# Adapter and conditional linear on one core: the up projection wholly from rounded parts, and a new order of work on four engines

## The chip, the cores and the metric

The kernel runs on one core of a Trainium2 chip. The metric is the device time of one execution in microseconds (us); smaller is better. Engines are named as in the profile: PE (TensorE, matrix products), PEld (its weight loads), DVE (VectorE), ACT (ScalarE), POOL (GpSimd), SP (SyncE, which here only issues DMAs). A q behind the name is the engine's own instruction queue.

## What is computed

For each of 32 samples x (512 tokens by 512 features), with weights picked by two id tables:

```
h      = relu(x @ W1[lang] + b1[lang])              # 512 -> 128, "up"
y      = x + h @ W2[lang] + b2[lang]                # 128 -> 512, "down"
normed = (y - mean(y)) * rsqrt(var(y) + 1e-5)
x1     = x + normed * gamma[lang] + beta[lang]
out    = x1 + x1 @ W[cat] + b[cat]                  # "linear"
```

## The kernel before

One sample is in work per step and three samples are in flight: step k does the adapter (up, relu, down, y, its sums) of sample k, the norm, its turning (transposes) and x1 of sample k-1, and the linear of sample k-2; it also prepares x and the adapter's weights of sample k+1 and splits W of sample k-1. There are steps 0 and 1 by hand, steps 2 to 31 from `step`, and an end. The class `Step` numbers the samples and the semaphore counts; `k.count(per, back, more)` is `per` times the index of sample k-back, plus `more`.

**Products by rounded parts.** An fp32 operand is split into a rounded part ("hi", type fp32r, made by ACT with a copy) and the remainder ("lo", made by POOL or DVE with a subtraction). `split_product` (lines 826 to 830) then issues three fp32r matmuls, hi by hi, hi by lo, lo by hi. The linear (12 matmuls for each of four token tiles, `linear_tile` at line 877), down (12, line 868) and the first NS = 3 of the four chunks of up (9, `up` at line 851) are done so. The fourth chunk of up is one plain fp32 matmul on the raw data, line 859, which the trace records as two.

**Order on each engine.** There is no planner: the five instruction lists are written out by hand and every wait is a semaphore. An engine works strictly in its own order. For step k:

- PE (line 889): linear tiles 0, 1 (sample k-2), up (k), turn norm chunks 0, 1 (k-1), linear tile 2, down (k), turn 2, 3 (k-1), linear tile 3. Linear tile 0 of a step waits, chunk by chunk, for x1T_lo of its sample (line 884), which DVE made in the step before.
- ACT (line 545): W's rounded half 0, four norms (k-1), W's half 1, relu (k) in two instructions (lines 518 and 521), two x-quad DMA issues for sample k+2, x1T_hi chunks 0, 1, then the hi parts of W2, W1 and x of sample k+1 (lines 476, 538, 543), squares 0 to 2 (line 527), x1T_hi 2, 3, square 3, the root (line 532).
- DVE (line 739): turn x of k+1 in four instructions (line 659) with outputs 0 and 1 (k-2) between, x1 0, the lo part of h, x1 1, x1T_lo 0, 1 (line 724), output 2, y and means of tiles 0, 1 and of 2, 3 (lines 673, 679), x1 2, 3, x1T_lo 2, 3, output 3, the variance and the inverse root in Newton steps (lines 691 to 710).
- POOL (line 387): identity added to W (line 395), b2 added to x tiles 0, 1 (line 413), W's lo half 0 (line 418), b2 on tiles 2, 3, W's lo half 1, the lo parts of W2, W1, x (lines 372, 378, 384).
- SP (line 276): three id loads into registers, two x-quad issues for k+2, then, behind a wait for the squares of sample k-1, W1 and W2 of k+1, W of k, b2 and x of k+1, b of k-1, half a store, and behind a wait for x1T_lo of k-1 the params (gamma, beta, b1) of k+1, and the other half store.

Relu of sample k waits for its params (line 515), since b1 is in them. The first square of a sample waits for y and its mean on DVE (lines 525, 526), the norms of a sample for its inverse root (line 485).

Of the kernel before, what the change touches and what calls it, by code (L numbers as in the profile page):

```python
# [36 lines left out]
def adapter_then_conditional_linear(nc, x, lang_ids, cat_ids, W1, b1, W2, b2, gamma, beta, W, b, out):  # L37
# [23 lines left out]
    P = 128  # L61
# [3 lines left out]
    NS = 3  # L65
# [17 lines left out]
    with ctx:  # L83
# [14 lines left out]
        b2_bc = [sb(f"b2_bc{i}", [P, H]) for i in range(2)]  # L98
# [34 lines left out]
        zeros = sb("zeros", [P, P])  # L133
        spare = sb("spare", [P, 4])
        ids = sb("ids", [1, 2, S], I32)
        param_rows = norm[0:L, :, :]
        param_table = sb("param_table", [P, L, NP])
# [7 lines left out]
        neg_mean_copy, var_eps, newton, newton2 = (d_bank[1][:, n * NT:(n + 1) * NT] for n in range(4))  # L145

# [85 lines left out]
        def _(sp):  # L232
# [3 lines left out]
            def load_x_quads(s, p, quads=(0, 1)):  # L236
# [17 lines left out]
            def load_b2(lang, p):  # L254
                sp.dma_start(b2_bc[p][:, :], b2[bass.ds(lang, 1)].to_broadcast([P, H])
                             ).then_inc(b2_in[p], 16)
# [19 lines left out]
            def step(h, p, quads=True, loads=True, w_load=True, turn=True, linear=True):  # L276
# [7 lines left out]
                if turn:  # L284
                    cat_b = sample_id(1, k.sample(1), G)
                if quads:
# [40 lines left out]
            load_b2(lang1, 1)  # L327
# [10 lines left out]
            load_x_quads(2, 0, range(NQ))  # L338
# [11 lines left out]
            last = Step(S // ROUND, 3)  # L350
            store(last, 2, 0)
# [10 lines left out]
        def _(pool):  # L362
# [24 lines left out]
            def step(h, p, adapter=True, turn=True, follow=True):  # L387
# [11 lines left out]
                def plus_b2(t):  # L399
# [5 lines left out]
                    pool.tensor_tensor(x_tok[p][:, t, :], x_tok[p][:, t, :], b2_bc[p][:, :],  # L405
                                       ALU.add).then_inc(x_b2_done, 1)

                def plus_b2_pair(t):
# [4 lines left out]
                    pool.tensor_tensor(pair, pair, b2_bc[p][:, :].rearrange("p (o h) -> p o h", o=1  # L413
# [56 lines left out]
        def _(act):  # L470
# [107 lines left out]
            def load_x_quads(s, p):  # L578
                for n in (2, 3):
                    act.dma_start(x_quad[p][quad(n), :, :],  # L580
                                  x_quads[bass.ds(s, 1), n].rearrange("o j b f -> j (o b) f")
# [416 lines left out]
```

## Time and profile before

| | us |
|---|---|
| median of 3 runs (lowest, highest) | 616.76 (616.46, 617.0) |
| profiled execution, its own time | 616.09 |
| span of that execution | 614.3 |
| PE busy | 607.1 (99%) |
| DVE, ACT, POOL busy | 523.2, 512.8, 524.0 |
| granted TensorE clock | 1.000 |

The span is counted from the first to the last instruction; 1.8 us of the time lie around it. Busy shares are averages over 32 samples, and a step repeats every 18.40 us, so the rows below are mostly those of one step in the middle (335.5 to 353.9 us). Each timeline row gives start, duration, engine and line, operation, operands, count, and in brackets the idle time ahead of it with what ended it. The same instruction returns 18.40 us later in the next step.

### The profile page before, as it was taken

The page shows a single profiled execution, that of the slowest core. Times are in us where ns is not written, and L with a number is a line of the kernel's source. Part 1 is how long each engine was busy: PE and PEld are TensorE (multiplying, and loading weights), DVE is VectorE, ACT ScalarE, POOL GpSimd, SP SyncE. Part 2 cuts the span into 40 slices and gives each one's busy share as a digit, 9 for nine tenths or more (in the row PEclk, how much of TensorE's full clock was granted, in tenths as well). Part 3 has the DMA queues.
Part 4 walks back from the last instruction along what each step waited for, and adds up shares of the span by engine and source line. Part 5 has one row for each costly group of instructions (what it writes and reads, how often), then busy time and mean ns, then how long its engine had stood idle before and what let it go on. Part 6 is the DMA issues. An engine that isn't in the chain of part 4 may idle for free.

```text
span 614.3 us, 10766 instructions
## 1 busy us (share of the span) xinstructions
PE 607.1 (99%) x2888; PEld 492.3 (80%) x2888; DVE 523.2 (85%) x1154; ACT 512.8 (83%) x769; POOL 524.0 (85%) x262
## 2 busy tenths in 40 slices
PE   9999999999999999999999999999999999999998
PEld 7767888888877888888888888888888888888887
DVE  1799899889799898898988998888898988998673
ACT  4768889889888889888989889889888989889770
POOL 4789999899889899889999888898988999888830
PEclk9999999999999999999999999999999999999999
DMA  9968998897997988989888998988998888998422
GB/s 308 247 206 272 307 305 275 278 296 250 307 297 251 301 271 281 318 270 292 274 287 280 306 297 258 287 280 273 313 290 280 281 287 275 300 306 276 154 85 104
DMA packets 125759, 166.24 MB, mean 271 GB/s; under 512 B 10882, under 2 KB 72588, under 8 KB 121632
## 3 DMA queue, kind: packets, MB, share of 16 engines
q1 hardware_dynamic: 94756, 150.12, 75.2%
q10 hardware_dynamic: 30972, 15.78, 9.2%
q8 instruction: 11, 0.18, 0.1%
q14 instruction: 20, 0.16, 0.1%
HBM read 132.17 MB, written 33.55 MB: 270 GB/s over the span
## 4 chain that ended last, share of the span: by engine, by line
PE 93%; DMA 2%; ACT 2%; DVE 2%; issue 1%; SPq 0%; POOL 0%; DVEq 0%; POOLq 0%; ACTq 0%
PE o_bank L828 18%; PE o_bank L830 18%; PE o_bank L829 18%; PE n_bank L846 9%; PE d_bank L828 5%; PE d_bank L830 5%; PE d_bank L829 5%; PE d_bank L859 5%; PE y_bank L828 2%; PE y_bank L830 2%; PE y_bank L829 2%; DMA x_tok<-in_x 2%; ACT norm L491 1%; PE y_bank L836 1%; DVE xT L659 1%
## 5 line engine op out<-in xcount | busy, mean ns | idle before, releaser
L828 PE MATMUL o_bank<-w_hi,x1T_hi 128*128 128x512 f32 x512 | 205.3, 401 | 0.8 <-DVE x1T_lo L724 0.8
L830 PE MATMUL o_bank<-w_hi,x1T_lo 128*128 128x512 f32 x512 | 200.0, 391 | 0.0
L829 PE MATMUL o_bank<-w_lo,x1T_hi 128*128 128x512 f32 x512 | 199.1, 389 | 0.0
L418 POOL TENSOR_TENSOR w_lo<-w_raw,w_hi 128x1024 fp32r<-128x1024 f32 x62 | 149.4, 2409 | 9.9 <-ACT w_hi L501 9.9
L659 DVE STREAM_TRANSPOSE xT<-x_quad 128x512 f32<-128x512 f32 x120 | 127.2, 1106 | 31.1 <-DMA x_quad<-in_x 31.1
L491 ACT ACTIVATE norm<-y,neg_mean_rstd,rstd 128x512 f32<-128x512 f32 x127 | 151.1, 1264 | 1.1 <-DVE neg_mean_rstd L709 1.1
L413 POOL TENSOR_TENSOR x_tok<-x_tok,b_bc 128x1024 f32<-128x1024 f32 x60 | 145.4, 2424 | 1.2 <-issue 1.1
L830 PEld LDWEIGHTS o_bank<-w_hi,x1T_lo 128*128 128x128 f32 x512 | 96.1, 188 | 21.0
L508 ACT ACTIVATE x1T_hi<-n_bank,params 128x512 fp32r<-128x512 f32 x126 | 84.6, 689 | 33.6 <-DVE n_bank L718 26.4
L828 PEld LDWEIGHTS o_bank<-w_hi,x1T_hi 128*128 128x128 f32 x512 | 96.3, 188 | 19.6 <-issue 1.7
L829 PEld LDWEIGHTS o_bank<-w_lo,x1T_hi 128*128 128x128 f32 x512 | 96.4, 188 | 17.8
L527 ACT ACTIVATE x_tok<-y,neg_mean 128x512 f32<-128x512 f32 x128 | 91.7, 718 | 17.4 <-DVE neg_mean L679 17.4
L384 POOL TENSOR_TENSOR xs_lo<-xT,xs_hi 128x1536 fp32r<-128x1536 f32 x29 | 102.1, 3522 | 0.0
L718 DVE SCALAR_TENSOR_TENSOR n_bank<-n_bank,params,xT 128x512 f32<-128x512 f32 x126 | 92.4, 757 | 10.3 <-PE n_bank L846 9.9
L724 DVE SCALAR_TENSOR_TENSOR x1T_lo<-n_bank,params,x1T_hi 128x512 fp32r<-128x512 f32 x126 | 90.8, 749 | 9.4 <-ACT x1T_hi L508 4.2
L736 DVE TENSOR_TENSOR out_half<-o_bank,b_bc 128x512 f32<-128x512 f32 x127 | 86.0, 677 | 11.8 <-PE o_bank L830 11.7
L501 ACT ACTIVATE w_hi<-w_raw 128x1024 fp32r<-128x1024 f32 x64 | 67.5, 1057 | 18.1 <-POOL w_raw L395 17.2
L372 POOL TENSOR_TENSOR w_lo<-w_raw,w_hi 128x512 fp32r<-128x512 f32 x31 | 40.4, 1303 | 47.6 <-ACT w_hi L476 47.6
L846 PEld LDWEIGHTS n_bank<-ident,norm 128*128 128x128 f32 x504 | 59.4, 145 | 9.0 <-ACT norm L491 1.1
L846 PE MATMUL n_bank<-ident,norm 128*128 128x128 f32 x504 | 65.7, 273 | 0.1
L395 POOL TENSOR_TENSOR w_raw<-w_raw,ident 128x512 f32<-128x512 f32 x32 | 50.5, 1577 | 0.0
L828 PE MATMUL d_bank<-xs_hi,w_hi 128*128 128x512 f32 x87 | 46.0, 529 | 0.0
(87 smaller groups left out, 821.2 us busy)
## 6 DMA issues: line engine op xcount, KB each, us to landing
w_raw<-in_L_cond_W SPq DMA_DIRECT2D x32, 1024.0 KB, 6.5
out<-out_half SPq DMA_DIRECT2D x63, 512.0 KB, 4.1
x_tok<-in_x SPq DMA_DIRECT2D x31, 1024.0 KB, 11.3
w_raw<-in_L_cond_W SPq DMA_DIRECT2D x64, 256.0 KB, 4.1
b_bc<-in_L_cond_b SPq DMA_DIRECT2D x64, 256.0 KB, 8.5
x_quad<-in_x SPq DMA_DIRECT2D x62, 256.0 KB, 3.7
x_quad<-in_x ACTq DMA_DIRECT2D x58, 256.0 KB, 10.7
x_tok<-in_x ACTq DMA_DIRECT2D x2, 256.0 KB, 3.3
```

Of the source, the lines that this page charges most:

```text
L384: pool.tensor_tensor(xs_lo[:, :, :], xT[(k.x + 1) % 3][:, 0:NS, :], xs_hi[:, :, :].bitcast(F32), ALU.subtract).then_inc(xs_lo_done, 1)
L413: pool.tensor_tensor(pair, pair, b2_bc[p][:, :].rearrange("p (o h) -> p o h", o=1).to_broadcast([P, 2, H]), ALU.add).then_inc(x_b2_done, 2)
L418: pool.tensor_tensor(w_lo[q][:, c:c + 2, :], w_raw[q][:, c:c + 2, :], w_hi[q][:, c:c + 2, :].bitcast(F32), ALU.subtract).then_inc(w_lo_don ...
L491: act.activation(dst, src, ACT.Identity, scale=rstd[:, t:t + 1], bias=neg_mean_rstd[:, t:t + 1]).then_inc(norm_done, 1)
L527: act.activation(x_tok[k.b][:, t, :], y[:, t, :], ACT.Square, bias=neg_mean[:, t:t + 1], accum_out=sq_sum[:, t:t + 1]).then_inc(sq_done, 1)
L659: dve.transpose(xT[(k.x + 1) % 3][:, c, :].rearrange("p (b j) -> p b j", j=SQ), x_quad[1 - k.b][:, :, c::NC]).then_inc(xT_done, 1)
L718: dve.scalar_tensor_tensor(norm_bank(k, c)[:, :], norm_bank(k, c)[:, :], params[q][:, c:c + 1], xT[(k.x + 2) % 3][:, c, :], ALU.mult, ALU. ...
L724: dve.scalar_tensor_tensor(x1T_lo[q][:, c, :], norm_bank(k, c)[:, :], params[q][:, NC + c:NC + c + 1], x1T_hi[q][:, c, :].bitcast(F32), AL ...
L828: pe.matmul(acc, lhs_hi, rhs_hi, start=first, stop=False)
L829: pe.matmul(acc, lhs_hi, rhs_lo, start=False, stop=False)
L830: return pe.matmul(acc, lhs_lo, rhs_hi, start=False, stop=last)
L846: ins = pe.transpose(norm_bank(k, c)[:, t * P:(t + 1) * P], norm[:, t, c * P:(c + 1) * P] if by_chunk(k) else norm[:, t, c::NC], ident[:, :])
```

## The change

- All four chunks of up go by rounded parts (NS = 4): the fp32 matmul becomes three fp32r ones, and the hi and lo parts of W1 and x are a third larger.
- ACT: three norms come ahead of W's half 0 and the fourth ahead of half 1; the hi part of W2 comes ahead of relu, those of x and W1 between relu and x1T_hi 0; the four squares and the root come ahead of x1T_hi 2 and 3. ACT issues no x quads.
- DVE: variance and inverse root come ahead of x1T_lo 2, 3 and output 3.
- POOL: both b2 additions come ahead of W's lo halves, the first also ahead of the identity; the lo part of x comes ahead of that of W1.
- SP: issues all four x quads; params of sample k are loaded in step k, behind W and x (before: in step k-1); the half store moves on to the next step; b2 has one buffer and is loaded last, after POOL has added the b2 of sample k. The steps have four id loads instead of three.
- `zeros` (used by the idle matmuls of the start) lies in an output buffer.

```diff
-    NS = 3
+    NS = 4
...
-        b2_bc = [sb(f"b2_bc{i}", [P, H]) for i in range(2)]
+        b2_bc = sb("b2_bc", [P, H])
...
-        zeros = sb("zeros", [P, P])
+        zeros = out_half[1][:, 1, 0:P]
...
+        def b2_of(k):
+            return b_bc[1] if k.since(1) and not k.since(2) else b2_bc
... SP, load_x_quads
-                for n in quads:
+                for n in range(NQ):
... SP, step
+                if w_load and k.since(2):
+                    lang_now = sample_id(0, k.sample(0), L)
                 if quads:
                     sp.wait_ge(xT_done, k.count(NC, 0, NC))
                     load_x_quads(k.sample(-2), p)
...
                     load_w(cat_w, p)
                 if loads:
-                    load_b2(lang, q)
                     load_x(k.sample(-1), q)
+                if w_load and k.since(2):
+                    sp.wait_ge(x1_lo_done, k.count(NC, 1, 0))
+                    load_params(lang_now, p)
+                if linear and k.since(3):
+                    store(k, 3, 1)
                 if turn:
...
                 if linear:
                     store(k, 2, 0)
                 if loads:
-                    sp.wait_ge(x1_lo_done, k.count(NC, 0, 0))
-                    load_params(lang, q)
-                if linear:
-                    store(k, 2, 1)
+                    sp.wait_ge(x_b2_done, k.count(NT, 0, NT))
+                    load_b2(lang, q)
... POOL, step
+                    if adapter and not k.last(2):
+                        plus_b2_pair(0)
                     if turn:
                         plus_identity()
-                    if adapter:
+                    if adapter and k.last(2):
                         plus_b2_pair(0)
-                    if turn:
-                        low_w_pair(0)
                     if adapter:
                         plus_b2_pair(2)
                     if turn:
+                        low_w_pair(0)
                         low_w_pair(2)
                 if follow:
                     low_w2(q, k.count(1, -1, 1))
                     if k.since(2):
+                        low_xs(k)
                         low_w1(k)
-                        low_xs(k)
... ACT, step
-                if k.last(2):
-                    for t in range(NT):
-                        normalise(k, t)
-                    high_w(k, 0)
-                else:
-                    high_w(k, 0)
-                    for t in range(NT):
-                        normalise(k, t)
+                for t in range(NT - 1):
+                    normalise(k, t)
+                high_w(k, 0)
+                normalise(k, NT - 1)
                 high_w(k, 2)
+                if follow:
+                    high_w2_of_next(k)
                 if adapter:
                     relu(k)
-                if follow and not k.last(S - 2):
-                    load_next_x_quads(k)
+                if follow:
+                    high_xs_of_next(k)
+                    high_w1_of_next(k)
                 high_x1(k, 0)
                 high_x1(k, 1)
-                if follow:
-                    high_w2_of_next(k)
-                    high_w1_of_next(k)
-                    high_xs_of_next(k)
                 if adapter:
-                    square(k, 0)
-                    square(k, 1)
-                    square(k, 2)
+                    for t in range(NT):
+                        square(k, t)
+                    deviation(k)
                 high_x1(k, 2)
                 high_x1(k, 3)
-                if adapter:
-                    square(k, 3)
-                    deviation(k)
... DVE, step
                 x1(k, 3)
+                if adapter:
+                    variance(k)
+                    inverse_deviation(k)
                 low_x1(k, 2)
                 low_x1(k, 3)
                 output(k, 3)
-                if adapter:
-                    variance(k)
-                    inverse_deviation(k)
... PE, up
-                                        False, c == parts - 1)
+                                        c == 0 and parts == NC, c == parts - 1)
```

## Rows read from the trace of the kernel before

**Rows 1.** One step in the middle, windows view: busy time of each engine

```profile
335.51:353.91 18.40, 18.40 (x88) 14.99 (x88) 17.59 (x39) 16.23 (x25) 16.72 (x9) 1.00 0.89 285
```

The columns are the stretch, its length, then PE, PEld, DVE, ACT and POOL busy with instruction counts, the granted clock, the DMA share and GB/s.

**Rows 2.** Timeline of PE in that step: up, and the turning behind it

```profile
335.34 1.02 PE L859 MATMUL d_bank<-xT,w_raw 128*128 128x512 f32 x2
...
336.43 0.39 PE L829 MATMUL d_bank<-xs_lo,w_hi 128*128 128x512 f32 x1
...
338.28 1.03 PE L846 MATMUL n_bank<-ident,norm 128*128 128x128 f32 x8
```

**Rows 3.** Groups over the span: operands, count, busy us, mean ns

```profile
L384 POOL TENSOR_TENSOR xs_lo<-xT,xs_hi 128x1536 fp32r<-128x1536 f32 x29 | 102.1, 3522 | 0.0
...
L543 ACT ACTIVATE xs_hi<-xT 128x1536 fp32r<-128x1536 f32 x29 | 43.0, 1481 | 0.0
...
L378 POOL TENSOR_TENSOR w_lo<-w_raw,w_hi 128x384 fp32r<-128x384 f32 x29 | 29.6, 1020 | 0.0
```

**Rows 4.** Timeline of ACT in that step

```profile
338.48 0.66 ACT L518 ACTIVATE d_bank<-d_bank,params 128x512 f32<-128x512 f32 x1 [0.17 <-PE d_bank L830]
339.17 0.60 ACT L521 ACTIVATE hT_hi<-d_bank 128x512 fp32r<-128x512 f32 x1
...
340.66 1.27 ACT L508 ACTIVATE x1T_hi<-n_bank,params 128x512 fp32r<-128x512 f32 x2 [0.89 <-DVE n_bank L718]
341.82 0.63 ACT L476 ACTIVATE w_hi<-w_raw 128x512 fp32r<-128x512 f32 x1
342.34 0.52 ACT L538 ACTIVATE w_hi<-w_raw 128x384 fp32r<-128x384 f32 x1
342.75 1.49 ACT L543 ACTIVATE xs_hi<-xT 128x1536 fp32r<-128x1536 f32 x1
344.77 0.72 ACT L527 ACTIVATE x_tok<-y,neg_mean 128x512 f32<-128x512 f32 x1 [0.53 <-DVE neg_mean L679]
...
349.09 0.30 ACT L532 ACTIVATE std<-sq_sum,eps 128x4 f32<-128x4 f32 x1
349.90 1.06 ACT L501 ACTIVATE w_hi<-w_raw 128x1024 fp32r<-128x1024 f32 x1 [0.51 <-POOL w_raw L395]
```

**Rows 5.** Timeline of ACT in the last adapter step, which prepares no next sample

```profile
577.69 0.66 ACT L518 ACTIVATE d_bank<-d_bank,params 128x512 f32<-128x512 f32 x1 [0.18 <-PE d_bank L830]
...
580.41 0.69 ACT L508 ACTIVATE x1T_hi<-n_bank,params 128x512 fp32r<-128x512 f32 x1 [0.66 <-DVE n_bank L718]
583.86 0.72 ACT L527 ACTIVATE x_tok<-y,neg_mean 128x512 f32<-128x512 f32 x1 [2.76 <-DVE neg_mean L679]
```

**Rows 6.** Timeline of DVE in the step of the middle, its end

```profile
347.74 1.41 DVE L724 SCALAR_TENSOR_TENSOR x1T_lo<-n_bank,params,x1T_hi 128x512 fp32r<-128x512 f32 x2
...
349.79 0.17 DVE L700 RECIPROCAL r<-std 128x4 f32<-128x4 f32 x1
...
350.60 0.16 DVE L709 TENSOR_TENSOR neg_mean_rstd<-d_bank,rstd 128x4 f32<-128x4 f32 x1
```

**Rows 7.** DMA view of stretches that hold one issue: W late alone, then x, b

```profile
w_raw<-in_L_cond_W SPq DMA_DIRECT2D x1, 1024.0 KB, 4.8
...
x_tok<-in_x SPq DMA_DIRECT2D x1, 1024.0 KB, 10.5
...
b_bc<-in_L_cond_b SPq DMA_DIRECT2D x1, 256.0 KB, 10.8
```

The last column is the time from issue to landing in us; W was issued at 572.92, x at 337.86 and b at 338.46.

**Rows 8.** Windows view: W, b and a store without x quads, then two stretches with x quads

```profile
575.00:579.00 4.00, 4.00 (x22) 3.24 (x21) 1.21 (x2) 3.77 (x5) 4.00 (x3) 1.00 1.01 403
337.30:343.30 6.00, 6.00 (x32) 4.98 (x31) 5.73 (x9) 4.91 (x9) 4.32 (x3) 1.00 1.06 329
...
22.00:24.00 2.00, 1.10 (x9) 0.86 (x7) 0.86 (x2) 1.73 (x3) 2.00 (x3) 1.00 1.16 240
```

**Rows 9.** Timelines of the start: SP's first quads of step 2, ACT's relu of sample 2

```profile
39.77 0.87 SPq L238 DMA_DIRECT2D x_quad<-in_x  x2
...
41.94 0.66 ACT L518 ACTIVATE d_bank<-d_bank,params 128x512 f32<-128x512 f32 x1 [1.45 <-PE d_bank L859]
```

More of the change, by code:

```diff
@@ L234, in sample_id, with load_x_quads @@
                 return sp.value_load(ids[0:1, which, bass.ds(s, 1)], min_val=0, max_val=count - 1)
-            def load_x_quads(s, p, quads=(0, 1)):
-                for n in quads:
+            def load_x_quads(s, p):
+                for n in range(NQ):
                     sp.dma_start(x_quad[p][quad(n), :, :],
@@ L252, in load_w2, with load_b2 @@
                              ).then_inc(w2_in[p], 16)
-            def load_b2(lang, p):
-                sp.dma_start(b2_bc[p][:, :], b2[bass.ds(lang, 1)].to_broadcast([P, H])
+            def load_b2(lang, p, dst=b2_bc):
+                sp.dma_start(dst[:, :], b2[bass.ds(lang, 1)].to_broadcast([P, H])
                              ).then_inc(b2_in[p], 16)
@@ L326, in _ @@
             lang1 = sample_id(0, 1, L)
-            load_b2(lang1, 1)
+            load_b2(lang1, 1, b_bc[1])
             load_w1(lang1, 1)
@@ L336, in _ @@
             load_params(lang1, 1)
-            load_x_quads(2, 0, range(NQ))
+            load_x_quads(2, 0)
             step(0, 1, linear=False)
@@ L350, in _ @@
             last = Step(S // ROUND, 3)
+            store(last, 3, 1)
             store(last, 2, 0)
@@ L404, in plus_b2 @@
                             pool.wait_ge(first_xT_turned, k.count(NC, 0, NC))
-                    pool.tensor_tensor(x_tok[p][:, t, :], x_tok[p][:, t, :], b2_bc[p][:, :],
+                    pool.tensor_tensor(x_tok[p][:, t, :], x_tok[p][:, t, :], b2_of(k)[:, :],
                                        ALU.add).then_inc(x_b2_done, 1)
@@ L412, in plus_b2_pair @@
                     pair = x_tok[p][:, t:t + 2, :]
-                    pool.tensor_tensor(pair, pair, b2_bc[p][:, :].rearrange("p (o h) -> p o h", o=1
+                    pool.tensor_tensor(pair, pair, b2_of(k)[:, :].rearrange("p (o h) -> p o h", o=1
                                        ).to_broadcast([P, 2, H]), ALU.add).then_inc(x_b2_done, 2)
@@ L547, in step @@
                 k = Step(h, p)
-                if k.last(2):
-                    for t in range(NT):
-                        normalise(k, t)
-                    high_w(k, 0)
-                else:
-                    high_w(k, 0)
-                    for t in range(NT):
-                        normalise(k, t)
+                for t in range(NT - 1):
+                    normalise(k, t)
+                high_w(k, 0)
+                normalise(k, NT - 1)
                 high_w(k, 2)
+                if follow:
+                    high_w2_of_next(k)
                 if adapter:
                     relu(k)
-                if follow and not k.last(S - 2):
-                    load_next_x_quads(k)
+                if follow:
+                    high_xs_of_next(k)
+                    high_w1_of_next(k)
                 high_x1(k, 0)
                 high_x1(k, 1)
-                if follow:
-                    high_w2_of_next(k)
-                    high_w1_of_next(k)
-                    high_xs_of_next(k)
                 if adapter:
-                    square(k, 0)
-                    square(k, 1)
-                    square(k, 2)
+                    for t in range(NT):
+                        square(k, t)
+                    deviation(k)
                 high_x1(k, 2)
                 high_x1(k, 3)
-                if adapter:
-                    square(k, 3)
-                    deviation(k)
[L578 to L581, printed above, removed]
-                                  ).then_inc(xq_in[p], 16)
-            def load_next_x_quads(k):
-                act.wait_ge(xT_done, k.count(NC, 0, NC))
-                load_x_quads(k.sample(-2), k.b)
             act.dma_start(x_tok[0][:, 1, :], x_rows[0, :, 1, :]).then_inc(first_x_in[1], 16)
@@ L627, in _ @@
             high_w2_of_next(k1)
-            load_next_x_quads(k1)
             for p in range(2, 2 + ROUND):
@@ L642, in _ @@
             STATS = 5
-            dve.memset(zeros[:, :], 0.0).then_inc(zeros_done, 1)
+            dve.memset(zeros, 0.0).then_inc(zeros_done, 1)
             dve.memset(spare[:, 0:1], 0.0).then_inc(out_done, OUT_CREDIT)
@@ L835, in keep_clock @@
                 for _ in range(count):
-                    pe.matmul(idle_bank[:, 0:P], zeros[:, :], zeros[:, :], start=True, stop=True)
+                    pe.matmul(idle_bank[:, 0:P], zeros, zeros, start=True, stop=True)
             def turn_norm(k, c):
```

## The prediction, made before the changed kernel ran

> **What bounds the kernel now.** I read the windows view of one step first, then the timelines of PE, ACT and DVE in that step, the groups, and last the DMA view. In the step of the middle PE is busy for all of its 18.40 us, while ACT has 16.23 us of work and POOL 16.72 [rows 1]. So a step costs what PE's list costs, and every other engine has a gap that costs nothing. ACT's gaps are the brackets of [rows 4]: 0.17 us for up, 0.89 for x1, 0.53 for the first mean, 0.51 for W with the identity. The question for a reordering is whether each engine's waits still fit into a step once its order is another. The profiled execution took 616.09 us against a median of 616.76; my sum is made against 616.09, and 0.2% (some 1.2 us) is about what a measurement of this kernel can tell from no change.
>
> **PE.** The fp32 chunk starts at 335.34; the first lo-matmul behind it starts at 336.43, which holds the chunk and one fp32r matmul. From 336.43 to the turning at 338.28 eight fp32r matmuls start, 0.231 us each [rows 2]. The chunk thus costs 1.09 - 0.23 = 0.86 us, its three fp32r matmuls 0.69. PE's list becomes 18.40 - 0.86 + 0.69 = 18.23 us: 0.17 less in each of 29 steps (3 to 31), 4.9 us if PE stays the bound.
>
> **ACT and POOL work.** Rounding 1536 columns of x takes 1.481 us [rows 3] and 384 of W1 0.52 [rows 4], so 0.84 ns a column; 512 and 128 more columns cost 0.43 + 0.11 = 0.54 us. ACT has then 16.23 + 0.54 = 16.77 us of work. On POOL the slope is (3.522 - 1.020)/1152 = 2.17 ns a column [rows 3], 640 more cost 1.39 us, and POOL has 18.11 us of work, just under PE's 18.23. POOL overlaps its instructions slightly, which the busy time of [rows 1] already holds.
>
> **The gap on ACT that loses its filler.** This is the largest term. The first square of a sample waits for its mean. That mean is behind x1T_lo 1, output 2 and two y tiles on DVE, and x1T_lo 1 waits for x1T_hi 1 on ACT. In [rows 4] x1T_hi 1 ends at 341.93 and the first square starts at 344.77, 2.84 us later. Before, ACT spends 2.3 us of this with the hi parts of W2, W1 and x, and only 0.53 shows as idle. The last step, which prepares no sample, shows the bare gap: from x1T_hi 1 at 580.41 to the square at 583.86, with 2.76 us idle [rows 5]. The change moves all three fillers ahead of x1T_hi 0 and puts nothing in their place; DVE's order between x1T_lo 1 and the mean stays. All of ACT's list lies on one closed loop (square, root, x1T_hi 2 and 3, norms, relu, hi parts, x1T_hi 0 and 1, gap, next square), so a step cannot be shorter than 16.77 + 2.84 = 19.6 us, whatever PE does. That excludes a gain unless one of the two numbers is wrong.
>
> **The loop through PE is a little longer.** Count from S, the end of the fourth square. The root ends 0.32 later (square's end 349.07 to root's end 349.39 [rows 4]). The inverse chain takes 0.97 from 349.79 to 350.76 [rows 6] and is now ahead of x1T_lo 2 and 3, whose two instructions take 1.41 [rows 6]: 0.32 + 0.05 + 0.97 + 1.41 = S + 2.75. Linear tile 0 of the next step then has its last three matmuls (0.69), tile 1 has 12 (2.77 at 0.231; I take 2.73, since such tiles run slightly faster than up), up has 12 (2.77), and 0.2 until relu starts: S + 9.15. ACT itself is there at S + 0.3 + 1.25 (x1T_hi 2, 3) + 6.8 (norms and W's two halves: 349.90 to the relu at 338.48 + 18.40 less its wait of 0.17) + 0.52 (W2) = S + 8.9, so PE's path is last by about 0.3.
>
> From relu to the next S: relu in two instructions 1.29, x 1.40 + 0.43, W1 0.41 + 0.11 (starts of neighbours in [rows 4]), x1T_hi 0 and 1 1.27, the gap 2.84, four squares 3.1 (344.77 to 349.09, less 1.25 for the x1T_hi 2 and 3 between them). That is 10.8, and the step 9.15 + 10.8 = 19.9 us. The cost on PE appears as a wait of linear tile 0 for x1T_lo 2, about 19.9 - 18.2 = 1.7 us a step. Slack elsewhere: the b2 buffer is released when POOL has added it, half a step ahead of the next use; x quads are issued from SP some 6 us after the last stores and needed a step later; output 3 ends as tile 1 needs its bank, with about 0.1 us to spare. I cost these at nothing; if one cover fails it adds its excess to the same loop, at most a few tenths. The wait of DVE for x quads disappears into slack. Taking the quad issues off ACT saves nothing, since they lay in its wait. The reordered POOL waits fit, as POOL has 1.8 us to spare in 19.9. The granted clock stays 1.00 even where PE worked 1.10 of 2.00 us [rows 8], so I add nothing for it.
>
> **The params.** SP now issues the params of sample k in step k, behind W1, W2, W and x of its own queue, and the W1 issue waits for the squares of k-1 (S). Relu of k waits for these params. In front of them lie 2.5 MB (2.62 million bytes). W alone landed 4.8 us after its issue [rows 7]; at the 403 GB/s of [rows 8] its 1.05 million bytes take 2.6, which leaves 2.2 of latency. So the params land at S + 0.05 + 2.2 + 6.5 = S + 8.75 at that rate, and at S + 10.2 at the 329 GB/s of the mixed stretch [rows 8]. I take the first, since x quads, which make the mixed stretches slow, have then landed; it is 0.4 ahead of PE's path, so it costs nothing in a steady step. The upper end would make the step 10.2 + 0.05 + 10.8 = 21.1. That a small transfer doesn't pass a large one of its queue I take from x and b: issued at 337.86 and 338.46 they landed at 348.4 and 349.3 [rows 7].
>
> The Trainium skill, page "DMA: Bandwidth & Descriptors", section "Queues, rings and completion order", says that on each engine descriptors are consumed in ring order, but also that completion is "not FIFO per issuing engine". By the first the sum is as above; by the second the params could come early, and only the next term would fall away. That the landings of x and b kept their order agrees with the first.
>
> **Once, at the start.** Step 2 has no lead: SP issues the quads of sample 4 at 39.77 when DVE has turned sample 2 [rows 9], now four of them, then W1, W2, W, x and only then the params of sample 2. Before, these had long landed and relu of sample 2 ran at 41.94 [rows 9]. Now 1.05 million bytes of quads at 240 GB/s (4.4 us; a stretch with many quads, [rows 8]), 2.62 million at 403 (6.5) and 2.2 latency put it at 52.9: 10.9 us later. Bounds: 9.3 with all at 403 GB/s, 11.5 with all at 329, nothing if params overtake.
>
> **Sum.** Relu of sample 2 to that of sample 31 is 577.69 - 41.94 = 535.75 us for 29 steps, 18.47 each. New: 29 x 19.9 = 577.1, 41.4 more. Behind the last relu PE has up finished about 0.5 us sooner relative to it. 616.1 + 10.9 + 41.4 - 0.5 = 667.9; I say 668.
>
> **Rivals.** (a) The params cycle decides: relu at S + 10.2 or later, steps of 20.5 to 21.1 us, 616.1 + 10.9 + 29 x (20.5 to 21.1 - 18.47) = 686 to 703. For it: most stretches of the trace are below 403 GB/s, and SP may be late. Against: those stretches are mixed with quads. 0.27. (b) The params overtake x (the page's second rule as it would act here): no loss at the start, steps of 19.6 to 19.9, so 616.1 + 33 to 41 = 649 to 657. Against it is the order of x and b. 0.08. (c) Faster: the swap in up decides, because the gap at the first square is covered. It wins if that gap is under 18.23 - 16.77 = 1.46 us instead of 2.84; the price is the 0.17 us of a step, and the time 616.1 - 4.9 = 611. For it: PE is the bound now and gets shorter, and the inverse root comes earlier. Against: [rows 5], where nothing but DVE's own list lies in the gap. 0.05. (d) Gap as in (c), but POOL's 18.11 us meet a wait and the step becomes 18.6: 620. 0.02.
>
> **How the numbers follow.** The forecast has 0.57 (660 to 680), (a) 0.27, (b) 0.08, (c) 0.05, (d) 0.02, the rest 0.01 beyond. The range reaches from 649, steps of 19.6 without the loss at the start, to 703, steps of 21.1 with it. Faster 0.05, within 0.2% 0.01, slower 0.94.
>
> **What would show it.** Right: steps of 19.9 us, ACT idle some 2.8 us in each ahead of the first square, waiting for the mean; PE idle 1.5 to 2 us a step at linear tile 0, waiting for x1T_lo; relu of sample 2 near 53 us with a wait for the params' DMA. Relu waiting for that DMA in every step is (a). An ACT without a wait of over 1.5 us ahead of the squares, and steps of 18.2, would prove the argument wrong.

## The result and the profile after

The changed kernel takes 747.0 us (742.41 to 750.75, 4 runs) against 616.63 us (616.46 to 617.0) before: 1.210 times as long [1.207, 1.214]. The forecast was 668 and the range ended at 703. The direction was right; the size was not. The profiled execution took 743.29 us, 127.2 more than the one of before, at a mean granted clock of 0.968.

Read first where the added time lies. Relu of sample 2 starts at 54.00 us (41.94 before), relu of sample 31 at 704.71. So 12.1 us are lost once at the start, and the 29 steps are (704.71 - 54.00)/29 = 22.44 us each against 18.47, which is 115.0 us. Together that is all but 0.2 of the 127.2; the rest lies behind the last relu. The page of the kernel after gives the busy times, and in its second fence line the shares of the chain that ended last:

```profile
PE 643.5 (87%) x2917; PEld 505.8 (68%) x2917; DVE 526.3 (71%) x1154; ACT 519.1 (70%) x769; POOL 561.9 (76%) x262
...
DMA 32%; ACT 23%; DVE 19%; PE 13%; issue 12%; SPq 1%; ACTq 0%; DVEq 0%
```

PE was busy for 99% of the span and is so for 87% now; PE's own work is only 13% of the chain. The largest share is DMA, all of it one item: the params. The waits, over the span (total us, times, longest), tell what this is:

```profile
ACT d_bank L528 <- DMA params<-param_table: 88.8, 27, 4.8
...
ACT x_tok L537 <- DVE neg_mean L669: 85.8, 31, 2.8
...
PE o_bank L818 <- DVE x1T_lo L714: 62.6, 30, 2.3
```

Line 528 is relu. It waits for the params in 27 of 32 samples, which the forecast had as rival (a). The second line is the gap ahead of the first square, the third is linear tile 0. One step on ACT, from relu to relu:

```profile
325.15 0.66 ACT L528 ACTIVATE d_bank<-d_bank,params 128x512 f32<-128x512 f32 x1 [3.68 <-DMA params<-param_table]
...
332.76 0.73 ACT L537 ACTIVATE x_tok<-y,neg_mean 128x512 f32<-128x512 f32 x1 [2.84 <-DVE neg_mean L669]
...
335.82 0.30 ACT L542 ACTIVATE std<-sq_sum,eps 128x4 f32<-128x4 f32 x1
...
343.99 0.61 ACT L486 ACTIVATE w_hi<-w_raw 128x512 fp32r<-128x512 f32 x1
347.32 0.66 ACT L528 ACTIVATE d_bank<-d_bank,params 128x512 f32<-128x512 f32 x1 [2.71 <-DMA params<-param_table]
```

Two stretches make the step. From relu to the end of the fourth square, S = 335.80, it is 10.65 us, and the gap of 2.84 us stands in it as forecast. From S to the next relu it is 11.52 us instead of 9.15. ACT is idle for the last 2.71 of these, and what ends the wait is the landing of the params. (PE too is late in this step, see the paragraph on the clock below.) SP's queue in the same step shows what is ahead of them:

```profile
335.95 0.36 SPq L251 DMA_DIRECT2D w_raw<-in_L_cond_W  x1
336.40 0.38 SPq L255 DMA_DIRECT2D w_raw<-in_L_cond_W  x1
336.97 0.33 SPq L267 DMA_DIRECT2D w_raw<-in_L_cond_W  x1
337.39 0.39 SPq L247 DMA_DIRECT2D x_tok<-in_x  x1
338.57 0.53 SPq L263 DMA_DIRECT2D params<-param_table  x1
339.36 1.01 SPq L277 DMA_DIRECT2D out<-out_half  x1
```

W1, W2, W and x go out within 1.8 us of S; the params go out at S + 2.8, when x1T_lo is ready. The DMA view of stretches that hold one of these issues each (last column: us to landing) gives their landings, and the chain names the one that ends last:

```profile
w_raw<-in_L_cond_W SPq DMA_DIRECT2D x1, 1024.0 KB, 6.9
...
x_tok<-in_x SPq DMA_DIRECT2D x1, 1024.0 KB, 9.7
...
params<-param_table SPq DMA_DIRECT2D x1, 4.5 KB, 8.7
```

```profile
338.57 8.66 DMA params<-param_table
```

x landed at 337.39 + 9.7 = 347.1, and the 4.5 KB of params at 338.57 + 8.66 = 347.2, that is S + 11.4: they land with the burst. So it is in all 27 steps that load an x: the params land 0.15 to 0.21 us behind it. The windows view says at what rate the burst came in:

```profile
336.00:337.20 1.20, 0.00 (x0) 0.00 (x0) 0.91 (x6) 1.20 (x4) 1.20 (x2) 1.00 0.00 0
...
337.60:347.20 9.60, 9.27 (x39) 7.60 (x39) 6.93 (x10) 7.00 (x7) 7.88 (x5) 0.82 0.94 312
...
339.00:341.50 2.50, 2.50 (x8) 1.95 (x7) 2.50 (x4) 2.50 (x3) 1.36 (x1) 0.60 0.86 246
...
343.00:344.50 1.50, 1.50 (x8) 1.22 (x7) 1.38 (x2) 1.50 (x3) 1.50 (x2) 1.00 0.83 202
344.50:347.10 2.60, 2.60 (x16) 2.21 (x15) 0.05 (x1) 0.10 (x1) 2.60 (x2) 1.00 1.04 383
```

No byte moves before 337.2. From about 337.4 to 347.1 the engines bring in the 2.62 million bytes, which is 270 GB/s; with the half store issued behind they move 312 in all, at 94% of their time. The forecast had 403 GB/s. The rate is uneven: 246 GB/s behind the landing of W2 (339.3), 202 around that of W (343.9), and 383 at the end, when W has landed and x is still on its way. This step is one of the quicker ones: over the span x takes 10.3 us to land (median), and the params land at S + 12.1 (median; 10.4 to 12.5 in the steps that load an x).

### The profile page after: what moved, and what is told of

Read it like the earlier page. It is cut to its first block, busy times and chain, and to the rows that moved or that the text cites. A ratio compares the mean times of both kernels' runs of the same rounds, so it can differ in the third digit from the quotient of the medians.

```text
span 741.5 us, 10909 instructions
## 1 busy us (share of the span) xinstructions
PE 643.5 (87%) x2917; PEld 505.8 (68%) x2917; DVE 526.3 (71%) x1154; ACT 519.1 (70%) x769; POOL 561.9 (76%) x262
## 4 chain that ended last, share of the span: by engine, by line
DMA 32%; ACT 23%; DVE 19%; PE 13%; issue 12%; SPq 1%; ACTq 0%; DVEq 0%
DMA params<-param_table 32%; ACT x_tok L537 7%; DVE x1T_lo L714 7%; ACT xs_hi L553 6%; DVE y L663 5%; DVE out_half L726 3%; ACT d_bank L528 3%; PE o_bank L818 2%; ACT x1T_hi L518 2%; PE o_bank L819 2%; PE o_bank L820 2%; ACT w_hi L548 2%; ACT std L542 1%; PE d_bank L849 1%; DVE r L690 1%
## 5 line engine op out<-in xcount | busy, mean ns | idle before, releaser
L818 PE MATMUL o_bank<-w_hi,x1T_hi 128*128 128x512 f32 x512 | 215.2, 420 | 62.6 <-DVE x1T_lo L714 62.6
L820 PE MATMUL o_bank<-w_hi,x1T_lo 128*128 128x512 f32 x512 | 206.7, 404 | 0.0
L819 PE MATMUL o_bank<-w_lo,x1T_hi 128*128 128x512 f32 x512 | 206.2, 403 | 0.0
L393 POOL TENSOR_TENSOR xs_lo<-xT,xs_hi 128x2048 fp32r<-128x2048 f32 x29 | 133.7, 4609 | 86.0 <-ACT xs_hi L553 86.0
L537 ACT ACTIVATE x_tok<-y,neg_mean 128x512 f32<-128x512 f32 x128 | 91.5, 716 | 85.8 <-DVE neg_mean L669 85.8
L819 PEld LDWEIGHTS o_bank<-w_lo,x1T_hi 128*128 128x128 f32 x512 | 100.8, 197 | 17.5
L726 DVE TENSOR_TENSOR out_half<-o_bank,b_bc 128x512 f32<-128x512 f32 x127 | 85.8, 676 | 13.9 <-PE o_bank L820 13.8
L528 ACT ACTIVATE d_bank<-d_bank,params 128x512 f32<-128x512 f32 x32 | 21.2, 662 | 98.2 <-DMA params<-param_table 88.8
L518 ACT ACTIVATE x1T_hi<-n_bank,params 128x512 fp32r<-128x512 f32 x126 | 79.1, 678 | 5.0 <-DVE n_bank L708 4.9
L836 PE MATMUL n_bank<-ident,norm 128*128 128x128 f32 x504 | 72.0, 278 | 0.1
L836 PEld LDWEIGHTS n_bank<-ident,norm 128*128 128x128 f32 x504 | 57.6, 145 | 19.1 <-DVE x1T_lo L714 13.7
L654 DVE TENSOR_TENSOR hT_lo<-d_bank,hT_hi 128x512 fp32r<-128x512 f32 x32 | 22.1, 692 | 68.0 <-ACT hT_hi L531 67.8
L553 ACT ACTIVATE xs_hi<-xT 128x2048 fp32r<-128x2048 f32 x29 | 55.3, 1905 | 0.0
## 6 DMA issues: line engine op xcount, KB each, us to landing
x_tok<-in_x SPq DMA_DIRECT2D x31, 1024.0 KB, 10.3
```

Of the source, the lines that this page charges most:

```text
L393: pool.tensor_tensor(xs_lo[:, :, :], xT[(k.x + 1) % 3][:, 0:NS, :], xs_hi[:, :, :].bitcast(F32), ALU.subtract).then_inc(xs_lo_done, 1)
L537: act.activation(x_tok[k.b][:, t, :], y[:, t, :], ACT.Square, bias=neg_mean[:, t:t + 1], accum_out=sq_sum[:, t:t + 1]).then_inc(sq_done, 1)
L726: dve.tensor_tensor(out_half[t // 2][:, t % 2, :], o_bank[t % 2][:, :], b_bc[k.b][:, :], ALU.add).then_inc(out_done, 1)
L818: pe.matmul(acc, lhs_hi, rhs_hi, start=first, stop=False)
L819: pe.matmul(acc, lhs_hi, rhs_lo, start=False, stop=False)
L820: return pe.matmul(acc, lhs_lo, rhs_hi, start=False, stop=last)
```

## The experiments

Read the results with this table. The profiled execution of each kernel is about 38 us, plus the start of relu of sample 2, plus 29 steps. Start and mean step are from relu's rows of that execution, whose own time can lie some us from the median (743.3 against 747.0 for the changed kernel). Relu is line 523, 526 or 529 in kernels whose lines have moved.

| | us (median) | relu 2 | step | ratio to before |
|---|---|---|---|---|
| before | 616.6 | 41.94 | 18.47 | 1 |
| after | 747.0 | 54.00 | 22.44 | 1.210 [1.207, 1.214] |
| params early | 667.0 | 48.38 | 20.02 | 1.084 [1.078, 1.090] |
| params early, NS = 3 | 658.7 | 48.52 | 19.68 | 1.068 [1.064, 1.071] |
| params between W and x | 669.4 | 50.89 | 20.00 | one run |
| params by ACT's queue | 709.8 | 49.07 | 21.44 | one run |
| gap filled, params late | 707.4 | 54.57 | 21.18 | one run |
| both mended | 645.6 | 49.08 | 19.23 | 1.044 [1.038, 1.050] |
| both, NS = 3 | 642.7 | 48.32 | 19.15 | 1.042 [1.038, 1.045] |
| both, identity first | 642.7 | 48.52 | 19.09 | 1.042 [1.040, 1.045] |
| all edits | 616.8 | 47.91 | 18.29 | 1.000 [0.999, 1.001] |
| all edits, start mended | 613.9 | 41.95 | 18.38 | 0.995 [0.994, 0.997] |
| all edits but params late | 731.2 | 53.69 | 22.05 | one run |

**Theory A**: two loops stacked on ACT's list, the params behind the burst and under them the gap ahead of the first square. **Rival B**: everything is on one queue, so moving 4.5 KB within it changes little. **Rival C**: the gap alone decides.

### Params ahead of W and x

```diff
                     load_w2(lang, q)
+                if w_load and k.since(2):
+                    sp.wait_ge(x1_lo_done, k.count(NC, 1, 0))
+                    load_params(lang_now, p)
                 if w_load:
...
                     load_x(k.sample(-1), q)
-                if w_load and k.since(2):
-                    sp.wait_ge(x1_lo_done, k.count(NC, 1, 0))
-                    load_params(lang_now, p)
```

> The changed kernel, with SP issuing the params of the step ahead of W and x instead of behind them. Theory A (the closed loop through the params transfer is the bound: squares of k-1 to the landing of the params of k 12 us, relu of k to its squares 10.6): relu no longer waits for a DMA; the step falls from 22.8 us to what PE's path gives, 19.9 if the granted clock stays at 1.00, 21.3 if it drops to 0.5 behind each wait as in the trace of the changed kernel; time about 668 to 710. Rival B (one DMA queue instead of two makes all loads slow and that is what is paid): the step stays at 22 us or more, about 740.

Measured: 667.0 us (666.26 to 672.4), 80 less, from moving one issue past two others. In the trace of this run the DMA view, and relu in two neighbouring steps:

```profile
params<-param_table SPq DMA_DIRECT2D x31, 4.5 KB, 1.7
```

```profile
330.17 0.66 ACT L528 ACTIVATE d_bank<-d_bank,params 128x512 f32<-128x512 f32 x1 [0.56 <-PE d_bank L820]
...
350.13 0.66 ACT L528 ACTIVATE d_bank<-d_bank,params 128x512 f32<-128x512 f32 x1 [0.57 <-PE d_bank L820]
```

The params land 1.7 us after their issue instead of 9.3, relu waits for PE alone, and the step is 19.96 us (mean 20.02). That is the step of the forecast's main case within about 0.1 us: it had assumed that the params cost nothing in a steady step and worked out 19.9. Rival B falls.

### Gap filled, params left late

```diff
                     relu(k)
+                high_x1(k, 0)
+                high_x1(k, 1)
                 if follow:
                     high_xs_of_next(k)
                     high_w1_of_next(k)
-                high_x1(k, 0)
-                high_x1(k, 1)
```

> The changed kernel, with ACT making x1T_hi 0 and 1 ahead of the hi parts of x and W1 of the next sample, so that these lie in its gap ahead of the first square; params still late. Theory A (both loops run through ACT's gap, so its filler shortens the params' loop too): relu to squares 10.6 less 2.3 = 8.3 us, plus 12 to the params, steps of 20.3 us, about 675. Theory C (ACT's unfilled gap alone explains the loss): steps of 18.2 to 18.6, about 611 to 622.

Measured: 707.41 us. In the waits of this run relu's wait for the params stays, and the gap is gone from ACT's timeline:

```profile
ACT d_bank L528 <- DMA params<-param_table: 71.7, 29, 4.9
```

```profile
550.43 0.73 ACT L537 ACTIVATE x_tok<-y,neg_mean 128x512 f32<-128x512 f32 x1 [0.44 <-DVE neg_mean L669]
```

Relu to S is 9.2 us there (544.27 to 553.48) instead of 10.65, but S to relu is 12.5. The gap alone is worth some 40 us of 130, so rival C falls; and the loop through the params bounds this kernel at 21.2 us a step. I had expected steps of 20.3 and 675 in all, a miss. Relu to S came out 0.9 us above the 8.3 expected, and 0.85 of this is a wait that the fillers used to hide. It now shows ahead of x1T_hi 1, for DVE's x1 1, which stands behind the lo part of h:

```profile
546.99 0.69 ACT L518 ACTIVATE x1T_hi<-n_bank,params 128x512 fp32r<-128x512 f32 x1 [0.85 <-DVE n_bank L708]
```

### Both, and both with up as before

The two diffs above together; then also `NS = 3`, which gives up its plain fp32 chunk back. That second kernel tells whether the swap in up is worth anything here.

> Both edits: params ahead of W and x, and ACT's gap filled. Theory A: no loop but PE's own list is left, steps of 18.23 us, and 611 to 614, if POOL's 18.11 us of work meet no wait; if POOL waits for the hi part of x, steps of 18.4 to 18.8, 617 to 628. Rival B: above 640.

> The two edits again, with NS back to 3: one chunk of up is plain fp32, and the hi and lo parts are a quarter smaller. If PE is the bound in both, this is 0.17 us a step slower than the kernel with both edits, by 4.9 us (0.8%); if POOL's list is the bound there, this one is faster than it, near 616.

Measured: 645.59 us (640.19 to 646.12) and 642.66 us (640.72 to 643.56). Both sit at steps of 19.2, well above PE's list (18.23 us, with NS = 3 18.40) and well above what was expected. The 2.9 us between their medians lie within their spreads, so the pair shows nothing for or against the swap in up while this loop is the bound. The two-by-two of these four kernels is: params alone -80, gap alone -40, both -101. The edits don't add, because each takes away one loop and the next longest takes over. The chain of the run with both edits names the third, here from one landing to the next:

```profile
297.94 9.48 DMA out<-out_half
...
307.51 0.08 DVE out_half L726
...
308.12 1.30 DVE y L663 x4
...
310.21 0.84 ACT x_tok L537 x3
...
314.53 0.75 DVE x1T_lo L714
...
315.40 0.51 SPq L263
...
317.26 9.05 DMA out<-out_half
```

The half store is issued behind the params (L263, which hold SP until x1T_lo is done), W and x, and takes 9 us to land. DVE can't write output 2 of the next step until it has, y stands behind output 2 in DVE's list, and the squares behind y. This item has 38% of the chain. The order of the same queue is at fault again, with the store in the place of the params, and the prediction did not have it.

### Identity ahead of b2 on POOL

```diff
-                    if adapter and not k.last(2):
-                        plus_b2_pair(0)
                     if turn:
                         plus_identity()
-                    if adapter and k.last(2):
+                    if adapter:
                         plus_b2_pair(0)
```

> The kernel with both edits (645.6 us, steps of 18.9), with POOL adding the identity to W ahead of b2 on tiles 0 and 1, as before the change. If the loop that is left runs through POOL (lo part of x, lo part of W1, b2, identity, W's hi half 0, norms, relu, hi part of x), it is 2.4 us shorter, and the next one decides, root to relu through PE 9.15 us and relu to squares 9.3: steps of 18.5, about 634. If the loop isn't there: no change within 0.3%.

Measured: 642.67 us (640.73 to 644.09), within the spread of the kernel it starts from. ACT's wait for POOL did vanish (9.5 us over 20 steps before the edit, 0.7 after) and bought nothing that can be told from the spread: a wait off the chain. The half store kept 35% of the chain. A miss.

### All edits

On top of that, three together: DVE does x1 1 ahead of the lo part of h; SP issues the half store ahead of W and x; in step 2 the hi part of W2 goes behind relu.

```diff
                     load_params(lang_now, p)
+                if linear and k.since(3):
+                    store(k, 3, 1)
                 if w_load:
...
                     load_x(k.sample(-1), q)
-                if linear and k.since(3):
-                    store(k, 3, 1)
...
-                if follow:
+                if follow and not k.last(2):
                     high_w2_of_next(k)
                 if adapter:
                     relu(k)
+                if follow and k.last(2):
+                    high_w2_of_next(k)
...
                 x1(k, 0)
+                x1(k, 1)
                 if adapter:
                     low_h(k)
-                x1(k, 1)
```

> As the run with the identity first, and besides: DVE makes x1 chunk 1 ahead of the lo part of h (ACT waits 0.67 us for it ahead of x1T_hi 1), SP issues the half store ahead of W and x (DVE waits up to 1.9 us for it), and in step 2 the hi part of W2 comes behind relu (it waits 7 us for its load there). Every loop is then under PE's list of 18.23 us, if I have them all: steps of 18.23, relu of sample 2 back near 42 us, and 611 to 613, 0.6% to 0.9% faster than before the change. If POOL's 18.1 us of work meet a wait: 618 to 625.

Measured: 616.82 us (615.94 to 618.41, 10 runs), ratio 1.000 [0.999, 1.001], some 4 us above the 611 to 613 expected. The steps came out as expected, the start did not. Relu in the middle, and at the start:

```profile
414.35 0.66 ACT L526 ACTIVATE d_bank<-d_bank,params 128x512 f32<-128x512 f32 x1 [0.56 <-PE d_bank L820]
...
432.63 0.66 ACT L526 ACTIVATE d_bank<-d_bank,params 128x512 f32<-128x512 f32 x1 [0.59 <-PE d_bank L820]
```

```profile
47.91 0.66 ACT L526 ACTIVATE d_bank<-d_bank,params 128x512 f32<-128x512 f32 x1 [7.46 <-DMA params<-param_table]
```

The steps are 18.2 to 18.3 us, which is PE's list of 18.23; PE has 95% of the chain and the half store none. Its median landing went from 8.3 to 5.5 us. By the chain it is the store edit that took away the 19.1 us loop, but the three edits were not run apart, so the share of the DVE edit is open. What the steps gain over before (29 x 0.18 = 5 us) the start gives back: relu of sample 2 waits 7.46 us for params that now stand behind four x quads.

### All edits, and the start mended

```diff
+                if w_load and k.last(2):
+                    sp.wait_ge(x1_lo_done, k.count(NC, 1, 0))
+                    load_params(lang_now, p)
                 if quads:
...
-                if w_load and k.since(2):
+                if w_load and k.since(2) and not k.last(2):
```

> The kernel with all edits (616.8 us, steps of 18.25, but relu of sample 2 at 47.9 us instead of 41.9, 7.5 us of it a wait for its params behind the quads), with the params of step 2 issued ahead of the quads of step 2. Relu of sample 2 returns to 41 to 42.5 us, the steps stay at 18.25: 610 to 612, 0.8% to 1.1% faster than before the change. If the loss at the start is made good later by PE's list anyway: no change, 616.8.

Measured: 613.9 us (613.41 to 615.47, 11 runs) against 617.23, ratio 0.995 [0.994, 0.997]. This version is 0.5% faster than the kernel before, and the interval keeps clear of no change. ACT at the start, then the windows view of one step:

```profile
41.95 0.66 ACT L529 ACTIVATE d_bank<-d_bank,params 128x512 f32<-128x512 f32 x1 [1.44 <-PE d_bank L852]
...
47.62 0.63 ACT L487 ACTIVATE w_hi<-w_raw 128x512 fp32r<-128x512 f32 x1 [4.37 <-DMA w_raw<-in_L_cond_W]
...
64.53 0.66 ACT L529 ACTIVATE d_bank<-d_bank,params 128x512 f32<-128x512 f32 x1 [0.52 <-PE d_bank L823]
```

```profile
300.00:318.25 18.25, 18.25 (x90) 15.13 (x89) 16.37 (x38) 16.62 (x25) 18.14 (x10) 1.00 0.95 286
```

Relu of sample 2 is back at its old time. But W2 for sample 3 is late behind the same quads, and that step takes 22.6 us, some 4 more than the others; so the gain is half of what was expected. In the steady step PE has no gap at all, and POOL is busy for 18.14 of 18.25 us: the new order leaves POOL 0.1 us of slack.

### Params late, all else mended

The reverse test: in the kernel with all edits the params go back behind W and x. I expected the params loop at its known length.

> The kernel with all edits, with the params behind W and x again, as in the changed kernel: that one part alone on a kernel whose other loops are short. Squares to params 11.5 to 12.2, relu to squares 8.6: steps of 20.1 to 20.8, with 6 us at the start some 675 to 695. If late params only hurt together with ACT's unfilled gap: steps of 18.3, 623.

Measured: 731.23 us (one run), 114 more from the place of one 4.5 KB load, and 36 above my upper end. Relu, and SP's queue:

```profile
409.78 0.66 ACT L526 ACTIVATE d_bank<-d_bank,params 128x512 f32<-128x512 f32 x1 [4.54 <-DMA params<-param_table]
```

```profile
418.73 0.38 SPq L255 DMA_DIRECT2D w_raw<-in_L_cond_W  x1
421.56 0.41 SPq L277 DMA_DIRECT2D out<-out_half  x1
```

Between the two issues SP is held for 2.4 us by the half store, which waits for output 3. That store is now ahead of W, x and the params in the queue. Relu to S fell to 8.35 us (409.78 to 418.13), and S to relu rose to 13.1 (to 431.25). The edit that mends one order lengthens the loop of another: I had priced the params as if SP's queue ahead of them were unchanged.

### Between W and x, and on ACT's own queue

Two tests of what sets the landing. In the first the params are issued behind W and ahead of x; in the second ACT issues them itself, on its own DMA queue, ahead of W's half 1, and SP no longer does:

```diff
                 normalise(k, NT - 1)
+                if adapter:
+                    lang_now = act.value_load(ids[0:1, 0, bass.ds(k.sample(0), 1)], min_val=0, max_val=L - 1)
+                    act.wait_ge(x1_lo_done, k.count(NC, 1, 0))
+                    act.dma_start(params[k.b][:, :],
...
                 high_w(k, 2)
```

> The changed kernel, with the params between W and x: 1.57 million bytes ahead of them instead of 2.62. If the bytes ahead set the landing (2.3 us and 290 GB/s, as x showed in the changed kernel), they land 7.7 us after the squares, 1.4 ahead of PE's path: no wait for them in a steady step, steps of 19.9 to 20.1, 668 to 675. If it is the whole burst that must end first (as the run on ACT's queue hints): landing 10 us or more after the squares, steps of 21.5 us or more, above 705.

> The changed kernel, with the params of the step issued by ACT ahead of W's half 1 instead of by SP behind W and x; the same transfer at about the same time, on the other queue. Theory A1 (the params are late because their queue serves in order and 2.6 million bytes lie ahead): they land within 2 to 4 us of their issue, relu waits for them under 1 us, steps near 20.3 us, 670 to 690. Rival A2 (the DMA engines are full, so that any transfer issued then waits): landing in 6 us or more after the issue, steps of 22 us or more, above 735.

Measured: 669.4 us with steps of 20.0, and 709.8 us with steps of 21.4. The DMA view of the first and of the second:

```profile
params<-param_table SPq DMA_DIRECT2D x31, 4.5 KB, 5.7
```

```profile
params<-param_table ACTq DMA_DIRECT2D x30, 4.5 KB, 6.8
```

With 1.57 million bytes ahead (W1, W2, W) the landing takes 5.7 us, with 2.62 million 9.3, with W1 and W2 alone 1.7. In each run the params land right behind the last large load ahead of them: 0.2 us behind x in the changed kernel, 0.2 us behind W here (0.15 to 0.32 in the 27 steps), while x lands 2.7 to 4.5 us later. Ahead of W and x they find W1 and W2 nearly in (W2 lands at S + 3.5, they at S + 4.5), and 1.7 us is what is left of a landing. Here they land near S + 8.4, just before PE's path, so this kernel runs like the one with early params. It is the bytes ahead that count, not the queue's length behind. The landing that I had expected was S + 7.7.

A queue of its own saves little: the params issued at 408.53 find W and x already issued on the other queue (W at 405.71, x at 406.14) and land 6.5 us later, 6.8 in the median. They are issued 1.2 us later than SP would (S + 4.0) and land at S + 10.75 instead of S + 12.1. They do get ahead of x: at 415.0 against 415.75 here, and in all 27 steps that load an x, by 0.1 to 1.6 us, where on SP's queue they never did. So neither branch of what was expected holds as it stands: not 2 to 4 us, and not steps of 22. The Trainium skill, page "DMA: Bandwidth & Descriptors", section "Queues, rings and completion order", says that an engine goes round its queues by packets, but also that the semaphore's increment lands only after every earlier write of that engine, across its queues. The first rule alone would let the params land early, and the second can hold them up behind what the engines have already taken in. This trace has a landing ahead of x and yet 6.8 us after the issue, so it shows neither rule acting alone, and no run here separates a late read from a late semaphore.

### Early params with the old up

```diff
-    NS = 4
+    NS = 3
```

> The changed kernel with params early (667.0 us, steps of 19.9), NS back to 3, so that 0.54 us of ACT's rounding (0.43 of it, and the W1 part 0.11, on the loop from relu to the squares) are gone and PE's up is 0.17 longer. If the loop through ACT's unfilled gap is the bound: steps of 19.9 - 0.54 + 0.17 = 19.5, 11 us less, 656. If PE's list decided: 0.17 a step slower, 672.

Measured: 658.7 us (658.05, 659.37), steps of 19.68. As expected, giving up its fp32 chunk back makes this order faster by 8 us (11 expected). PE's list isn't the bound there; the loop is, from relu over ACT's list and its gap to S, and from S over x1T_lo and PE to relu. The swap adds 0.54 us to ACT's part of it and takes 0.17 from PE's. So the swap is a loss as long as this loop is the longer one. Once PE's list is the bound it should be a gain, 18.25 against 18.40 us a step, but the kernel with all edits was not run with NS = 3.

## Why the prediction was wrong in size and right in sign

**PE, ACT and POOL work.** Right. PE's step with nothing in its way is 18.25 us (18.23 forecast), POOL's work 18.14 (18.11), ACT's 16.6 (16.77).

**The gap on ACT.** Right: 2.84 us in the row above, and 85.8 us over 31 squares. With the params out of the way, the loop that holds it gives steps of 20.0.

**The loop through PE.** Right: with early params 19.96 us against 19.9. That this kernel's 667.0 us also meet the 668 is luck: the 668 hold 10.9 us for late params at the start, which it doesn't have. It loses 6.4 us there for another reason (below), and some 3.4 us in 29 steps of 20.02 instead of 19.9. In the kernel after, relu to S took 10.65 us against 10.8.

**The params: the step that failed.** The text had them at S + 8.75, with S + 10.2 as upper end, and called them hidden by 0.4 us. They landed at S + 11.4 in the step above, at S + 12.1 in the median, and the mean step of 22.44 puts relu at S + 11.8 on average. The latency at the head was no error: first bytes came 1.5 us after the first issue, where I had 2.2 in all. The term for the burst was: 2.62 million bytes took 9.7 us, not 6.5. I had taken 403 GB/s from a stretch with W, b and a store, and 329 as the lower bound because a stretch with x quads held it. "The x quads have then landed" was true and didn't help: the burst ran at 270 without them. It is not x that is slow, as the 383 GB/s at its end show, but the stretches behind W2's landing and around W's. The trace of before has a stretch of that kind in the very load that the 403 came from, W issued at 572.92:

```profile
573.50:575.00 1.50, 1.50 (x8) 1.06 (x7) 0.24 (x1) 1.50 (x2) 1.50 (x1) 1.00 0.73 98
```

The first 1.5 us in which it moved bytes ran at 98 GB/s; I had booked them as latency, to be paid once ahead of the burst, and taken the rate from 575.00 on. In the burst such slow stretches lie inside it. What makes them slow no run here separates, so the cause of the low rate stays open. The row at 240 GB/s in [rows 8] was kept for the start alone; had it been the lower bound, the upper end would have been S + 13.2, steps of up to 24 us, and the range would have held the result. And a margin of 0.4 us under a term that ran from 8.75 to 10.2 was no margin. The error is worth (22.44 - 19.9) x 29 = 74 us, and the experiment with early params got back 80 by the medians and 76 between the profiled executions, of which 5.6 lie at the start (54.00 - 48.38) and 70 in the steps.

**Rival (a)** named the right mechanism and its sign, relu waiting for that DMA (27 of 32 samples), with 0.27. Its price carried the same wrong rates: its condition was a landing at S + 10.2 "or later", but its dearest step, 21.1 us, is that of S + 10.2. Rival (b) falls: on SP's queue the params never overtook x. The steps of rivals (c) and (d), 18.2 to 18.6 us, exist only in the kernels with all edits, where the gap is filled and two more loops are cut.

**The clock.** I had added nothing. After PE's idle time of 2.34 us at linear tile 0 it was granted 0.50, the lower of its two levels (1.2 GHz), for some 3 us:

```profile
337.93 0.76 PE L818 MATMUL o_bank<-w_hi,x1T_hi 128*128 128x512 f32 x1 [2.34 <-DVE x1T_lo L714]
338.49 0.63 PE L819 MATMUL o_bank<-w_lo,x1T_hi 128*128 128x512 f32 x1
338.92 0.63 PE L820 MATMUL o_bank<-w_hi,x1T_lo 128*128 128x512 f32 x1
```

```profile
340.00:340.80 0.80, 0.80 (x3) 0.61 (x3) 0.80 (x2) 0.80 (x1) 0.36 (x1) 0.50 0.99 297
```

Its matmuls start 0.43 us apart there instead of 0.23. Up ends 1.6 us later for it, so PE's path would have had relu at about 346.6, S + 10.8 instead of 9.15, still 0.7 ahead of the params: it cost nothing here. The argument from a stretch with scattered gaps [rows 8] didn't carry over. But the gap doesn't decide it alone. Of the 25 steps with 2.1 to 2.4 us of idle time at linear tile 0, 11 show the lower level behind it and 14 do not, such as the step before this one:

```profile
314.80 0.47 PE L818 MATMUL o_bank<-w_hi,x1T_hi 128*128 128x512 f32 x1 [2.35 <-DVE x1T_lo L714]
```

```profile
315.50:316.30 0.80, 0.80 (x6) 0.66 (x5) 0.80 (x2) 0.80 (x1) 0.80 (x1) 1.00 0.88 192
```

In two of the 11 (relu at 188.40 and 505.91) PE's path ended last, by 0.2 and 0.4 us; in the other nine the params landed later still.

**The start.** 12.1 us against 10.9, near, but with a cause left out. With early params relu of sample 2 is still at 48.38: ACT now has the hi part of W2 ahead of relu, and W2 comes behind the quads.

```profile
48.54 0.63 ACT L486 ACTIVATE w_hi<-w_raw 128x512 fp32r<-128x512 f32 x1 [7.12 <-DMA w_raw<-in_L_cond_W]
...
54.00 0.66 ACT L528 ACTIVATE d_bank<-d_bank,params 128x512 f32<-128x512 f32 x1 [4.83 <-DMA params<-param_table]
```

**A cover that was not listed.** The prediction listed the b2 buffer, the x quads and output 3 as slack costed at nothing; the half store, whose buffer DVE needs back for output 2, is not among them. In the kernel with early params (steps of 20 us) it has 5% of the chain, in steps of 19.2 us 38%.

## What to carry to other kernels

When a change puts a load that is needed within the step behind a burst on the same queue, count the bytes that will be in flight ahead of it, divide by the slowest rate that the trace shows, with the slow first stretch of a large load counted in, and set that landing against the loop it closes; here a queue of its own let it pass only the last 0.1 to 1.6 us of the burst. Look for the order in which each small transfer stands ahead of the large ones: here the same small load ahead of W and x instead of behind them was worth 62 us (gap filled), 80 (gap open) and 114 (all edits). Loops don't add: list all that close within a step, longest first, and expect each repair to give only the distance to the next.

## What was not expected of the hardware

- 4.5 KB on ACT's own queue took 6.8 us to land while 2 MB of SP's queue were in flight, against 9.3 on SP's queue behind them and 1.7 ahead of them. It landed 0.1 to 1.6 us ahead of x, which had been issued first.
- W1, W2, W and x together came in at 270 GB/s with the engines 94% busy; the mixture that held W, b and a store had shown 403. Within the burst it went from 202 to 383.
- Idle stretches of 2.1 to 2.4 us on PE were followed by some 3 us at a granted clock of 0.50 in 11 steps and by 1.00 in 14. In the kernel with early params the idle stretch is 1.44 us in the step at 342.95, and the stretch behind it shows 1.00:

```profile
343.00:344.00 1.00, 1.00 (x5) 0.78 (x6) 1.00 (x3) 1.00 (x2) 1.00 (x2) 1.00 0.79 303
```
